# Next chunk's scores and late keys moved into the even chunks' attention, a projection tile moved out of the second chunk's

## The reference

```python
q, k, v = split_heads(x @ Wq), split_heads(x @ Wk), split_heads(x @ Wv)     # x is layernormed
q, k = relu(q) + EPS, relu(k) + EPS
k_cumsum = jnp.cumsum(k, axis=2)
context = jnp.cumsum(jnp.einsum('bhnd,bhne->bhnde', k, v), axis=2)
D_inv = 1.0 / jnp.einsum('bhnd,bhnd->bhn', k_cumsum, q)
attn = jnp.einsum('bhnd,bhnde,bhn->bhne', q, context, D_inv)
x = x + (attn @ Wo + bo)
gate, y = fp4_linear(layernorm(x), w_gate), fp4_linear(layernorm(x), w_up)
x = x + fp4_linear(silu(gate) * y, w_down)
```

## Time and profile before

| | |
|---|---|
| Median of three runs | 1525.87 us |
| Span of the profiled execution | 1522.3 us |
| PE busy | 1491.0 us, 98% |
| DVE busy | 1183.0 us, 78% |
| POOL busy | 725.2 us, 48% |
| ACT busy | 650.7 us, 43% |

### The profile page before, as it was taken

The page is one execution under the profiler, slowest core; times in us unless marked ns, Lnnn a source line. Parts: engine busy times, 40 slices in busy tenths (PEclk is TensorE's granted clock), DMA queues, the critical chain, the costliest instruction groups (busy, mean ns, idle before and its releaser), DMA issues.

```text
span 1522.3 us, 55070 instructions
## 1 busy us (share of the span) xinstructions
PE 1491.0 (98%) x23652; PEld 1401.0 (92%) x23652; DVE 1183.0 (78%) x2322; ACT 650.7 (43%) x1165; POOL 725.2 (48%) x822
## 2 busy tenths in 40 slices
PE   8889999999999999999999999999999999999998
PEld 7878999999999999999999999999999999999998
DVE  8786777877878877778777778777778877878767
ACT  5434444343453444443343443444443343453433
POOL 4313555444555444554444554445554444554543
PEclk9999999999999999999999999999999999999999
DMA  4101233233233333233333233232233232233210
GB/s 168 34 2 43 85 102 109 77 97 95 83 104 100 88 95 96 77 110 92 89 103 92 85 105 96 86 102 86 84 113 101 79 103 89 81 112 92 82 51 15
DMA packets 159361, 133.27 MB, mean 88 GB/s; under 512 B 12944, under 2 KB 150672, under 8 KB 159120
## 3 DMA queue, kind: packets, MB, share of 16 engines
q1 hardware_dynamic: 159120, 129.75, 28.6%
HBM read 68.09 MB, written 61.60 MB: 85 GB/s over the span
## 4 chain that ended last, share of the span: by engine, by line
PE 81%; DVE 5%; DMA 3%; issue 2%; SPq 1%; ACT 1%; POOL 1%; DVEq 0%; POOLq 0%; ACTq 0%
PE bank L607 62%; PE bank L740 3%; PE bank L808 3%; PE bank L729 3%; PE bank L774 3%; PE bank L691 2%; DMA hq_away<-hq_blocks 1%; DMA attn_away<-probs 1%; PE bank L835 1%; PE bank L855 1%; PE bank L617 1%; PE bank L713 1%; PE bank L886 1%; SPq L563 0%; DVE probs L1835 0%
## 5 line engine op out<-in xcount | busy, mean ns | idle before, releaser
L1517 POOL TENSOR_TENSOR attnT_lo<-attn,attnT_hi 128x1024 fp32r<-128x1024 f32 x58 | 141.2, 2434 | 253.2 <-ACT attnT_hi L1200 253.2
L607 PE MATMUL bank<-xT_hi,wqk_hi 128*128 128x256 f32 x1024 | 211.1, 287 | 2.8 <-ACT qkT L1127 1.5
L607 PE MATMUL bank<-xT_hi,wqk_lo 128*128 128x256 f32 x1024 | 203.6, 280 | 0.0
L607 PE MATMUL bank<-xT_lo,wqk_hi 128*128 128x256 f32 x1024 | 203.4, 280 | 0.0
L1127 ACT ACTIVATE qkT<-bank 128x512 f32<-128x512 f32 x256 | 149.7, 595 | 113.6 <-PE bank L607 110.9
L1577 POOL TENSOR_SCALAR qkT<-qkT 128x512 f32<-128x512 f32 x256 | 158.4, 632 | 61.8 <-ACT qkT L1127 60.7
L607 PEld LDWEIGHTS bank<-xT_hi,wqk_hi 128*128 128x128 f32 x1024 | 157.1, 188 | 7.2 <-issue 3.8
L607 PEld LDWEIGHTS bank<-xT_lo,wqk_hi 128*128 128x128 f32 x1024 | 156.5, 188 | 0.0
L607 PEld LDWEIGHTS bank<-xT_hi,wqk_lo 128*128 128x128 f32 x1024 | 156.5, 188 | 0.0
L1250 ACT ACTIVATE silu<-bank 128x352 f32<-128x352 f32 x128 | 58.7, 459 | 222.5 <-PE bank L607 221.0
L1529 POOL TENSOR_TENSOR hqT_lo<-hq,hqT_hi 128x768 fp32r<-128x768 f32 x58 | 130.7, 2253 | 17.8 <-ACT hqT_hi L1215 17.6
(11 more groups left out here) (219 smaller groups left out, 3868.4 us busy)
## 6 DMA issues: line engine op xcount, KB each, us to landing
attn<-attn_away SPq DMA_DIRECT2D x232, 128.0 KB, 2.9
hq_away<-hq_blocks SPq DMA_DIRECT2D x58, 384.0 KB, 3.2
hq<-hq_away SPq DMA_DIRECT2D x232, 96.0 KB, 2.3
attn_away<-probs SPq DMA_DIRECT2D x58, 256.0 KB, 2.7
attn_away<-probs SPq DMA_DIRECT2D x116, 128.0 KB, 2.7
x_in<-in_L_attn_x SPq DMA_DIRECT2D x32, 256.0 KB, 2.8
out<-out_sb SPq DMA_DIRECT2D x64, 128.0 KB, 2.7
qkT<-in_L_attn_Wq SPq DMA_DIRECT2D x1, 1024.0 KB, 8.4
```

Source lines behind the costliest of these rows:

```text
L607: at = pe.matmul(dst, lhs_at(kt), rhs_at(kt), start=first and kt == 0, stop=last and kt == k_tiles - 1)
L1517: pool.tensor_tensor(by_raw_attn(attnT_lo), attn_raw, by_raw_attn(attnT_hi).bitcast(F32), ALU.subtract).then_inc(attnT_ready, 2)
```

## The change

In a steady step `between()` no longer holds a projection tile.

- In a first chunk it holds the late keys and the scores of the second chunk, which stood at the start of the second chunk's step.
- In a third chunk it holds the first half of the fourth chunk's `last_scores`.
- In a second chunk it is empty: the projection tile goes behind `attend`, ahead of the tile that stood there.

On DVE the second chunk's `add_late` goes to the first chunk's step, behind its `add_early`. In the odd steps `begin_h` is cut in two, and `add_early` goes between the halves. All banks of the steady steps are dealt anew. The number of instructions on each engine stays as it was. SP's list is the same.

```diff
         steady = {
-            "scores": [(5, 3), (3, 6), (6, 2), (2, 5, 7, 3)],
+            "scores": [(1, 0), (0, 1), (1, 6), (0, 1, 4, 7)],
...
-            "kv": [(0, 1), (3, 4), (4, 5), ()],
+            "kv": [(0, 1), (5, 6), (2, 3), ()],
...
-            "late_kv": [(), (1, 2), (3, 4), (0, 1)],
+            "late_kv": [(), (6, 7), (3, 4), (2, 3)],
...
+                steady = g >= WARM
+
                 def between():
-                    if project:
+                    if steady:
+                        if c == 0:
+                            late_keys(b, c + 1, g + 1)
+                            scores(b, c + 1, g + 1, u)
+                        elif c == 2:
+                            last_scores(b, c + 1, g + 1, u, (0,))
+                    elif project:
                         project_qk(b, c, u + 1, 0, 1)
...
-                if c:
+                if c and not (steady and c == 1):
                     late_keys(b, c, g)
                 if c < CHUNKS - 1:
-                    scores(b, c, g, u)
+                    if not (steady and c == 1):
+                        scores(b, c, g, u)
                     turn_k(b, c, g)
                 else:
-                    last_scores(b, c, g, u)
+                    last_scores(b, c, g, u, (1,) if steady else range(2))
...
-                        project_qk(b, c, u + 1, 2 * n + (c == 1 and n == 0), 2 * n + 2)
+                        project_qk(b, c, u + 1, 2 * n + (c == 1 and n == 0 and not steady), 2 * n + 2)
...
                 add_early(g)
+                if c == 0:
+                    add_late(g + 1)
...
-                add_late(g)
+                if c > 1:
+                    add_late(g)
...
-                begin_h(g - 3)
+                scales_of_h(g - 3)
                 if c < CHUNKS - 1:
                     add_early(g)
+                scaled_h(g - 3)
```

More of the change, by code:

```diff
@@ L279, in build_program @@
         steady = {
-            "x": [(0,), (), (7,), ()],
-            "scores": [(5, 3), (3, 6), (6, 2), (2, 5, 7, 3)],
-            "k": [(1, 6), (4, 7), (0, 1), ()],
-            "xq": [(4,), (4,), (5,), (0,)],
-            "v": [(2, 7), (5, 0), (7, 3), (6, 0)],
-            "kv": [(0, 1), (3, 4), (4, 5), ()],
-            "av": [(3, 4, 5, 6), (6, 7, 1, 2), (6, 7, 0, 1), (1, 2, 4, 5)],
-            "gate_up": [(7, 4, 5, 0), (7, 3, 5, 2), (5, 3, 6, 4), (4, 5, 3, 7)],
-            "late_kv": [(), (1, 2), (3, 4), (0, 1)],
-            "qk": [(), (5, 0, 5, 6, 4, 6, 0, 1), (), (7, 3, 7, 1, 6, 1, 2, 4)],
-            "wo": [(3,), (2,), (6,), (2,)],
-            "down": [(1,), (5,), (2,), (7,)],
+            "x": [(5,), (), (7,), ()],
+            "scores": [(1, 0), (0, 1), (1, 6), (0, 1, 4, 7)],
+            "k": [(3, 4), (5, 6), (2, 5), ()],
+            "xq": [(2,), (2,), (0,), (6,)],
+            "v": [(6, 7), (7, 2), (7, 1), (5, 6)],
+            "kv": [(0, 1), (5, 6), (2, 3), ()],
+            "av": [(2, 3, 4, 5), (0, 1, 3, 4), (4, 5, 6, 7), (0, 1, 2, 3)],
+            "gate_up": [(7, 2, 3, 4), (0, 1, 3, 4), (3, 4, 5, 6), (0, 2, 3, 6)],
+            "late_kv": [(), (6, 7), (3, 4), (2, 3)],
+            "qk": [(), (5, 6, 5, 6, 5, 6, 2, 5), (), (4, 7, 4, 7, 4, 7, 0, 4)],
+            "wo": [(7,), (2,), (5,), (6,)],
+            "down": [(7,), (0,), (1,), (2,)],
         }
@@ L966, in step @@
                 project = c % 2 == 1
+                steady = g >= WARM
                 def between():
-                    if project:
+                    if steady:
[5 more added lines that the diff above has]
+                    elif project:
                         project_qk(b, c, u + 1, 0, 1)
-                turned_late = g >= WARM and c % 2 == 1
+                turned_late = steady and c % 2 == 1
                 if c % 2 == 0 and g <= WARM:
@@ L1932, in gated_by_silu, with scales_of_h @@
                                   ALU.mult).then_inc(hid_ready, 1)
-            def begin_h(g):
+            def scales_of_h(g):
                 if g:
@@ L1938, in begin_h, with scaled_h @@
                             h_scale_ready, h_inv_ready, g)
+            def scaled_h(g):
                 round_scale(h_scaled_of(g), hid[:], h_inv[:], HB, h_inv_ready, h_scaled_ready, g)
+            def begin_h(g):
+                scales_of_h(g)
+                scaled_h(g)
             def round_h(g):
```

## The result

The changed kernel takes 1537.03 us (median of four runs, 1535.58 to 1540.49) against 1525.76 us of the kernel before beside it. The ratio is 1.0076, with a 95% interval of 1.006 to 1.0093: slower by 11.3 us, where 1531 was forecast, in a range of 1517 to 1539. The profiled execution has a span of 1536.2 us, 13.9 more than before, and its own time is 1537.97 us.

A forecast was written before the change was run, and what follows sets the result against it. The prediction took PE, busy 98% of the span, as the bound. Its terms, -4.4 - 5.3 - 2.8 + 0.5 + 18.0 = +6.0 us on 1522.3, gave a span of 1528.3 and a stated 1531 us, range 1517 to 1539.

The forecast's parts named there:

- Edges: PE's switches between small and large products at the two moved parts: 4.4 and 5.3 us off in 15 sequences.
- the block: Late keys and scores leaving the second chunk's start: edges of 0.29 us saved in each of 15 sequences, 4.4 us.
- the tile: Projection tile leaving the second chunk's attention: edges of 0.35 us saved in each of 15 sequences, 5.3 us.
- The longer runs: Longer runs of small products on PE: 23.6 stops for instructions, 19 more, adding 18.0 us.
- The count of 125 records: One instruction transfer holds 125 PE records; PE runs dry only in small-product runs longer than that, about 1 us each.
- First chunk's waits: PE's waits for `add_early` in first chunks mostly go under the late keys: 2.8 us off, ends 0 and 3.4.
- The second chunk's state: Without the tile as cover, `add_early` arrives just in time for the second L808: 0.5 us added, ends 0 and 15.
- The banks: Banks dealt anew in the steady steps only add waits on operations long done, but for one named: no cost.
- The sum: -4.4 - 5.3 - 2.8 + 0.5 + 18.0 = +6.0 us: span 1528.3, median 1531.9, stated as 1531 us.
- the Trainium skill's rule: Instruction fetch is mostly hidden by PE's 2048-instruction buffer, so longer runs cost nothing: sum -13 us.
- the stops don't multiply: Faster rival: PE's issue stops are something else or the fetch runs further ahead; -12 us, 1514 us, chance 0.18.
- come to 12 only: No-change rival: 12 more stops on PE instead of 19, -12 + 12 = 0, 1526 us, chance 0.22.

The follow-up runs named there:

- misaligned: As aligned, with 28 small products at the very start instead of 1; 1568.1 us, ratio 1.0275.
- aligned: Changed kernel with third-chunk value and feed-forward input banks moved, 60 groups of scores products issued twice, one small product at the start; 1519.41 us, ratio 0.9957.
- before_pads: Kernel before, with 60 groups of scores products issued twice in first chunks and one small product at the start; 1526.92 us, ratio 0.9987.
- before_aligned: Kernel before, with the first 8 scores products issued twice in the first chunks 24, 40 and 56; 1527.05 us, ratio 1.0001.

## Why the prediction was right

- **Edges.** Forecast 0.29 + 0.35 = 0.64 us a sequence. Measured, from L729 to L729, 0.23 (the block but its effect on L729), 0.39 (the tile, and that effect) and 0.05 in the third leg, 0.67 together. Right.
- **The longer runs.** Forecast 23.6 stops, 19 more than by the same count before, +18.0 us; measured from 9 to 29, 20 more, +17.7 us. By chunks 11.9, 4.2 and 7.5 were forecast; of the 27 largest 11 stand in first chunks, 7 in second, 8 in third, and 1 in a fourth, where none was forecast. The mechanism is shown by misaligned and aligned. Where PE ate its 256 instructions in 5 us or more, as a rule nothing was lost, but for the late starts above; in runs of small products an end of a packet cost up to 1.5 us in the changed kernel, and 1.9 to 2.0 at the worst place of three other runs. The Trainium skill, "Runtime: NRT & Kernel Launch", section "Instruction fetch mechanics", calls the crossing mostly hidden: the traces agree for the large products and not for the small. The count of 125 records, though, is only a good proxy. What counts is the time since the last packet was begun: the large products on both sides belong to it.
- **First chunk's waits.** Forecast 2.8 us off, with 0 to 3.4 as ends; 0.9 came off (3.4 to 2.5). The late keys cover only part of the wait, because PE asks for the state's bank 0.47 us after L774 and `add_early` often ends later than that.
- **The second chunk's state.** Forecast just in time, 0.5 us; one wait of 0.2 us. Right.
- **The banks.** "The new banks only add waits on operations long done" is the step that failed: 7 waits for the mask, 5.0 us. I had compared what stands in a bank with what stood before in the program, and not with when DVE is through in the worst of the third chunks. Its late masks were to be seen in the trace before, at no cost there.
- **The sum.** 1528.3 was forecast for the span, and 1536.2 came. The two misses, 5.0 of the banks and 1.9 of the first chunks' waits, are 6.9 of the 7.9 us. The median missed the sum's own 1531.9 by less, 5.1 us, because the runs lie 0.8 us above the span now and not 3.6. That is luck: it tells how the profiled execution lay among the others, and nothing of the change. The 1531 us stated was missed by 6.0. One sum of the prediction is off: the terms without the longer runs give -12 us, as its rivals have it, and not the -13 beside the Trainium skill's rule. The rivals by which the stops don't multiply, or come to 12 only, fell with the count.

## What to carry to other kernels

A run of cheap instructions has a second price beside its products: its length in instructions. Before merging two runs, count the instructions on that engine from one fetch to the next in the time that they take; where they take under about 3 us, a stop of about a microsecond comes with each fetch, and a merge that saves 0.3 us an edge can lose. The places are fixed by the program, so that a few dozen instructions more can move them out of the runs, for all sequences if one sequence is a whole number of fetches long. That was worth some 22 us to the changed kernel and nothing to the kernel before, which had few stops to lose, paid 7 us for the added products and got four late fetches. And a bank that is dealt anew must be held against the latest end of the operation that empties it, over all repetitions, not against one of them.

## What the runs showed of the hardware

- 27 small products more at the start changed the time by 48.7 us, from 1519.4 to 1568.1, and some 43 us of that lie in steps whose code was the same. Comparisons of two kernels whose instruction counts differ ahead of the loop carry this with them.
- A copy of DVE from one place of its memory to another, 0.29 us alone, waits to the end of a POOL operation that has begun, and ends 0.15 us after it: 18 of 28 times in the kernel before, 11 after. The Trainium skill, "SBUF — State Buffer", section "Who interferes with whom", says that a DVE cast that runs in a two-port mode and a GpSimd instruction exclude each other for the whole instruction, and that whoever is issued first goes first. No row tells the mode of this copy, but in what it does the trace agrees: where the copy began 0.03 us before POOL's operation, at 1333.21 us after, it took 0.30 us.
- The fetch of instructions sometimes starts 3.0 to 4.7 us after the packet before was begun, and not 0.8: for 4 stops of before_pads, 3 of before_aligned, 2 after and 1 before. In the 2 after other data moved meanwhile; from 453.1 to 456.8 us in before_pads none did. The cause is open.
